# A selective-state recurrence with experts woven in: B and C are split 0.3 turns later, the experts' tiles are placed anew, and a product of zeros goes ahead of each state's sum

## The reference, cut to what matters

```python
xi, z = split(x @ in_proj.T)            # inner width 256 in layer 1
xc = silu(conv(xi))                     # over 4 steps of time
dt, B, C = split(xc @ x_proj.T)         # 8, 16 and 16 numbers per token
delta = softplus(dt @ dt_w.T + dt_b)
for t in time:                          # 16 states for each of 256 rows
    h = exp(delta[t] * A) * h + (delta[t] * xc[t]) * B[t]
    y[t] = sum_n h[:, n] * C[t, n]
out = ((y + xc * D) * silu(z)) @ out_proj.T
# experts: S = sigmoid(x @ Wg).T ; G, I = top_k(S, 1024)
# hid = gelu(x[I] @ W1 + b1) ; new_x[I] += (hid @ W2 + b2) * G
```

## Time and profile before

| | us |
|---|---|
| median of three runs | 4028.96 |
| profiled execution, own time | 4031.42 |
| its span, first to last instruction | 4030.1 |
| second layer's recurrence and experts | about 850 to 2207 |
| fourth layer's recurrence | about 2540 to 2900 |

### The profile page before, as it was taken

One profiled execution on the slowest core, in us unless ns is written; L12 is line 12 of the kernel. 1 busy time (PEld: TensorE's weight loads), 2 busy tenths in 40 slices (PEclk: granted clock), 3 DMA queues, 4 the chain that ended last, 5 costly groups with the idle time before them and its releaser, 6 DMA issues.

```text
span 4030.1 us, 40714 instructions
## 1 busy us (share of the span) xinstructions
PE 3097.7 (77%) x14760; PEld 1359.4 (34%) x14850; DVE 2581.5 (64%) x2891; ACT 2028.4 (50%) x3628; POOL 1557.2 (39%) x938
## 2 busy tenths in 40 slices
PE   5788877975567777777775879777687888888876
PEld 2111212341222222232322644322234554554544
DVE  4676662439998888888787334577625655555563
ACT  1454453134456766766664211576435565555654
POOL 2211100113457667666657002244414443443432
PEclk7788897986778888887777979888698998999998
DMA  3221200021111221121111001001000000000000
GB/s 86 41 33 30 45 3 0 0 75 39 26 35 37 42 51 32 40 49 36 32 34 45 1 0 64 21 21 32 11 0 19 19 19 10 19 19 10 19 10 31
DMA packets 79733, 114.60 MB, mean 28 GB/s; under 512 B 16270, under 2 KB 49422, under 8 KB 78106
## 3 DMA queue, kind: packets, MB, share of 16 engines
q1 hardware_dynamic: 68268, 103.33, 10.7%
q0 software_dynamic: 11264, 8.66, 1.6%
HBM read 37.96 MB, written 17.33 MB: 14 GB/s over the span
## 4 chain that ended last, share of the span: by engine, by line
PE 49%; DVE 21%; ACT 16%; issue 7%; POOL 3%; DMA 2%; SPq 1%; POOLq 0%; DVEq 0%; ACTq 0%
DVE layer_mamba_state L1340 7%; PE psum L1112 3%; DVE psum L1328 3%; PE psum L2460 3%; ACT layer_mamba_decay L1266 3%; PE psum L1189 3%; PE psum L2491 3%; PE psum L779 2%; ACT layer_exps L792 2%; PE psum L236 2%; PE psum L248 2%; PE psum L2154 2%; PE psum L905 2%; PE psum L242 2%; PE psum L2544 2%
## 5 line engine op out<-in xcount | busy, mean ns | idle before, releaser
L1369 POOL TENSOR_TENSOR layer_mamba_state<-layer_mamba_state,layer_mamba_c 128x1024 f32<-128x1024 f32 x320 | 781.0, 2450 | 591.3 <-DVE layer_mamba_state L1340 585.1
L1340 DVE TENSOR_TENSOR_SCAN layer_mamba_state<-layer_mamba_decay,psum 128x1024 f32<-128x1024 f32 x320 | 731.4, 2286 | 43.7 <-ACT layer_mamba_decay L1266 11.5
L1189 PE MATMUL psum<-layer_mamba_state,two_to_one 128*64 128x512 f32 x1280 | 442.9, 784 | 124.1 <-DVE layer_mamba_x L1357 80.9
L1266 ACT ACTIVATE layer_mamba_decay<-layer_mamba_delta_wide,layer_weights 128x511 f32<-128x511 f32 x640 | 415.7, 711 | 76.1 <-DMA layer_mamba_delta_wide<-layer_mamba_delta 39.5
L1328 DVE TENSOR_TENSOR psum<-psum,layer_mamba_u_wide 128x1024 f32<-128x1024 f32 x320 | 393.3, 1229 | 62.0 <-PE psum L1147 26.0
L720 DVE TENSOR_REDUCE layer_peak<-psum 128x2 f32<-128x1024 f32 x256 | 306.6, 1218 | 112.7 <-PE psum L691 108.6
L792 ACT ACTIVATE layer_exps<-psum 128x1024 f32<-128x1024 f32 x256 | 250.8, 1029 | 222.6 <-PE psum L759 222.6
L2857 POOL TENSOR_TENSOR layer_p<-layer_p,layer_stats 128x512 f32<-128x512 f32 x128 | 133.2, 1041 | 299.0 <-DVE layer_stats L2780 298.8
L2651 ACT ACTIVATE layer_p<-psum,layer_stats 128x128 f32<-128x128 f32 x512 | 181.5, 369 | 130.1 <-DVE layer_stats L2773 129.6
L2844 POOL TENSOR_TENSOR layer_qk<-layer_qk,layer_v_between 128x1024 f32<-128x1024 f32 x64 | 150.5, 2351 | 216.1 <-DVE layer_v_between L2744 214.3
L1147 PE MATMUL psum<-layer_mamba_bc,layer_mamba_pick 96*64 96x512 bf16 x768 | 164.2, 455 | 87.5 <-DVE psum L1328 63.7
(11 more groups left out here) (349 smaller groups left out, 6185.8 us busy)
## 6 DMA issues: line engine op xcount, KB each, us to landing
layer_mamba_delta_wide<-layer_mamba_delta SPq DMA_DIRECT2D x160, 128.0 KB, 2.4
layer_mamba_u_wide<-layer_mamba_work SPq DMA_DIRECT2D x160, 128.0 KB, 2.4
layer_v_between<-layer_v SPq DMA_DIRECT2D x16, 512.0 KB, 4.3
qk_dram<-layer_qk_parts SPq DMA_DIRECT2D x16, 384.0 KB, 3.0
layer_q_rows<-qk_dram SPq DMA_DIRECT2D x96, 64.0 KB
layer_k_rows<-qk_dram SPq DMA_DIRECT2D x96, 64.0 KB
layer_v_between<-layer_v SPq DMA_DIRECT2D x16, 384.0 KB, 5.6
layer_weights<-weights_dram SPq DMA_DIRECT2D x1, 4147.0 KB, 12.2
```

The source lines that it names most:

```text
L1189: e = pe.matmul(c.psum[j * HALF:(j + 1) * HALF, self.sum_banks[h], :], c.two_to_one[:, :], self.state[i % len(self.state)][:, j, :], start ...
L1266: e = act.activation(decay[:, j, 1:SEQ], self.delta_wide[h][:, j, 1:SEQ], ACT.Exp, scale=rates[:, rate:rate + 1])
L1340: dve.tensor_tensor_scan(state, decay, self.fill.rearrange("p j t -> p (j t)"), 0.0, ALU.mult, ALU.add).then_inc(self.scanned, 1)
L1369: pool.tensor_tensor(state, state, self.both(self.c_wide[turn % self.C_BUFFERS][:, :]), ALU.mult).then_inc(self.multiplied, 1)
```

## The change: what it does

Three edits, all of them in the order and in one added product.

1. In the second layer's plan `split`, `cast` and `rest` go from 4.75, 4.9, 5.05 to 5.05, 5.2, 5.4 turns. The fourth layer's plan keeps its numbers.
2. `ROWS_AT`, `TURN_AT`, `PAIR_AT` and `GIVE_AT` have new numbers (and `COUNT_AT` differs in the second decimal place). The last `GIVE_AT` is 1047.75 in place of 1037.75, and with it all gates are planned 10 us later.
3. `pe_keep_up` issues, ahead of each item's sum and ahead of its wait, a bf16 product of a 128x128 tile of zeros with a column of zeros read 512 times. It accumulates into a sum bank that is open (a unit's first item has none open and gets no product): 240 in the second layer, 56 in the fourth, where the class is used too. POOL clears `zeros16` once at the start.

```diff
+        pool.memset(c.zeros16[:, :], 0.0).then_inc(made, 1)
+        c.constants = 17
...
         for turn, h, i, now in self.items(self.plan.sum):
             yield now
             unit, m = divmod(turn, TURNS)
+            self.pe_keep_up()
             hold.wait_ge(self.multiplied, i + 1)
...
             e.then_inc(self.summed, 1)
+            self.open[h] = m < TURNS - 1
+
+    def pe_keep_up(self):
+
+        if any(self.open):
+            self.c.pe.matmul(self.c.psum[:, self.sum_banks[self.open.index(True)], :], self.c.zeros16[:, :],
+                             self.c.zeros16[:, 0:1].broadcast_to([P, SEQ]), start=False, stop=False)
...
-    ... z_gate=3.8, proj=4.2, keep=4.5, split=4.75, cast=4.9, rest=5.05, dt=4.9,
+    ... z_gate=3.8, proj=4.2, keep=4.5, split=5.05, cast=5.2, rest=5.4, dt=4.9,
...
-TURN_AT = [214.5, 264.5, 314.5, 370.75, 420.75, 470.75, ...
+TURN_AT = [214.5, 264.5, 314.5, 370.75, 432.0, 482.0, ...
```

More of the change, by code:

```diff
@@ L180, in __init__ @@
         buf = lambda n, s, d=F32: c.buffer(c.ctx, n, s, d)
-        c.ident, c.ident16 = buf("ident", [P, P]), buf("ident16", [P, P], BF16)
+        c.ident, c.ident16, c.zeros16 = buf("ident", [P, P]), buf("ident16", [P, P], BF16), buf("zeros16", [P, P], BF16)
         c.mean_of, c.eps = buf("mean_of", [P, P]), buf("eps", [P, 1])
@@ L202, in pool @@
         pool.tensor_tensor(c.two_to_one[:, :], c.ident[:, 0:P // 2], c.ident[:, P // 2:P], ALU.add).then_inc(made, 1)
-        c.constants = 16
+        pool.memset(c.zeros16[:, :], 0.0).then_inc(made, 1)
+        c.constants = 17
         hold.wait_ge(made, c.constants - 1)
@@ L1012, in __init__ @@
         self.halves, self.taps, self.units, self.names = halves, taps, units, names
-        self.plan, self.banks, self.sum_banks = plan, banks, sum_banks
+        self.plan, self.banks, self.sum_banks, self.open = plan, banks, sum_banks, [False] * halves
         self.fill = c.psum[:, fill_bank:fill_bank + 2, :]
@@ L1401 @@
     start=48.0, pace=8.3, item=3.75, first=0.55, spread=-4.2, c_spread=-2.8, copy=-1.8, decay=-6.0,
-    conv=((2.45, 2.63), (2.81, 2.99)), x=(2.9, 3.22), z=3.5, z_gate=3.8, proj=4.2, keep=4.5, split=4.75, cast=4.9, rest=5.05, dt=4.9,
+    conv=((2.45, 2.63), (2.81, 2.99)), x=(2.9, 3.22), z=3.5, z_gate=3.8, proj=4.2, keep=4.5, split=5.05, cast=5.2, rest=5.4, dt=4.9,
     soft=5.15, log=5.75, u=(6.15, 6.35), send_delta=(6.5, 6.6), send_u=(7.17, 7.62), multiply=3.9, sum=16.0, y=1.6, gate=1.78,
     back=2.0, out=2.3)
-ROWS_AT = [30.0, 34.0, 38.0, 42.0, 46.0, 50.0, 54.0, 58.0]
-COUNT_AT = [12.0, 18.3, 24.6, 30.9, 37.2, 43.5, 49.8, 56.1, 62.4, 69.7, 78.0, 84.3, 94.6, 100.9, 107.2, 113.5, 119.8]
+ROWS_AT = [30.0, 35.5, 39.5, 43.5, 47.5, 51.5, 55.5, 59.5]
+COUNT_AT = [12.0, 18.3, 24.6, 30.90, 37.2, 43.5, 49.8, 56.09, 62.39, 69.69, 77.99, 84.29, 94.59, 100.89, 107.19, 113.49, 119.79]
 SPOT_AT = COUNT_AT[15] + 16.0
@@ L1409 @@
 LIST_AT = [141.75, 158.25, 167.25, 176.25, 185.25, 194.25, 208.0, 224.75]
-TURN_AT = [214.5, 264.5, 314.5, 370.75, 420.75, 470.75, 520.75, 570.75, 628.0, 678.0, 728.0, 778.0, 835.5, 885.5, 935.5, 985.5]
-PAIR_AT = [232.75, 242.75, 297.25, 307.25, 325.0, 363.75, 377.0, 387.0, 430.0, 440.0, 496.5, 506.5, 525.25, 562.75, 576.25, 586.25, 632.5, 642.5, 695.75, 705.75, 762.0, 772.0, 789.75, 828.5, 842.0, 852.0, 894.75, 904.75, 961.25, 971.25, 990.0, 1027.75]
-GIVE_AT = [252.75, 317.25, 373.75, 412.25, 450.0, 516.5, 572.75, 611.5, 652.5, 715.75, 782.0, 838.5, 877.0, 914.75, 981.25, 1037.75]
+TURN_AT = [214.5, 264.5, 314.5, 370.75, 432.0, 482.0, 532.0, 582.0, 636.5, 697.75, 747.75, 802.5, 852.5, 902.5, 963.25, 1013.25]
+PAIR_AT = [232.75, 242.75, 297.25, 307.25, 325.0, 363.75, 377.0, 387.0, 436.5, 446.5, 496.5, 506.5, 562.75, 572.75, 590.5, 629.25, 642.75, 652.75, 702.25, 712.25, 762.0, 772.0, 828.5, 838.5, 857.0, 894.75, 908.25, 918.25, 967.75, 977.75, 1027.75, 1037.75]
+GIVE_AT = [252.75, 317.25, 373.75, 429.0, 456.5, 516.5, 582.75, 639.25, 694.5, 722.25, 782.0, 848.5, 904.75, 960.0, 987.75, 1047.75]
 class Setup1:
```

## The result

The changed kernel took 4046.73 us (median of seven, 4040.64 to 4048.79), the kernel before 4026.98 in seven of its own. The ratio is 1.0041, 95% interval 1.003 to 1.0052: slower by 0.41%, some 17 us. I had forecast 4037 with a range of 4004 to 4060. The profiled execution has a span of 4047.4 us against 4030.1. All times here are medians of each kernel's executions. The kernel before had medians of 4027 to 4033 us in the series that follow, so kernels are compared by their ratio to it.

What follows compares the result with a forecast made beforehand. Twelve 78.0 us units were taken as bound by an engine-to-engine chain (42.6 us), then DVE (about 35). Terms 13 + 4 - 5 - 3 - 1 = +8 on the median of 4028.96 gave 4037, range 4004 to 4060.

Steps and rivals of the forecast that it cites:

- Chain and second part: Each of twelve 78.0 us second-layer units: 42.6 us engine-to-engine chain from gate to delta, then about 35 us bound by DVE.
- Split: Second layer's split of B and C: fill L1328 moves into L1302's wait; nothing gained in steady units, -1 us allowed elsewhere.
- Fill comes through: Rival, chance 0.12: L1314's wait is set by DVE's own earlier work through a buffer, so -15 us, 4022.
- Zeros on the chain, +13: Second layer, gate to delta: three products of zeros a unit cost 1.07 us, +13 over twelve units.
- Zeros elsewhere, 0: Other eight or so products of zeros a unit run beside DVE's part, in PE's 9.7 us idle; cost 0.
- Zeros and the clock, -3: PE's two idle stretches a unit: one in twenty-four stays warm through the zeros, saving 2.6 us, so -3.
- Experts placed anew, -5: Experts' pieces L1704: at ends of units 5, 9, 13 they may keep the clock up, -3; pieces leaving the chain, -2.
- Tail, +4: Recurrence's end, bound by POOL: last piece and experts' gates planned 10 us later; +4 us, bounds 0 and +10.
- Fourth layer, 0: Its 56 products of zeros cost 0, bounds -2 and +4; PE waits for ACT ahead of dt there.
- Clock held: Rival, chance 0.20: half of the 24 cold PE stretches turn warm, -31 in place of -3, 4009.
- PE late in DVE's part: Rival, chance 0.15: zeros delay spreads behind the delta, +26 us, 4063; sign: L1337 waits for L1148 in the second part.
- POOL's backlog: Rival, chance 0.13: POOL's blocked fetch of 17.46 us moves to another unit, prolonging it by slow L1316s; +8, 4045.

## Why the prediction was right, and where it was not

The forecast was slower by 8 us, it became 17, inside a wide range. That the number held is in part luck, for the place was wrong. My terms put +5 us into the twelve chains (zeros +13, clock -3, boundaries -3, pieces that leave -2) and nothing into the second parts; measured are +1.7 and +14.6. By the sign that I had set myself, the second part moving from 35 us, the forecast's account is wrong: its mean went from 35.2 to 36.5. By its steps:

- **Chain and second part.** The division carried the whole study: the twelve units hold 16.2 of 17.3 us.
- **Split.** Right. The fill ran in L1302's wait (3.2 to 1.7 us a unit) and about half of it came back in L1314's (2.5 to 3.2, where I had 3.7). "Fill comes through" is out: with the new tables and no zeros the chain is 1.5 us shorter with the moved split than without it, not 15, and the ratio shows nothing.
- **Zeros on the chain, +13.** Right with the new tables: 501.4 to 514.1 is +12.7. With the old ones it is +6.1, so the hit is not the proof of a fixed price of three products a unit. The single product was mis-sized a little: at the lower clock the next row starts after 0.54 us (1390.07 to 1390.61), not 0.43:

```profile
1390.07 0.61 PE L1199 MATMUL psum<-zeros 128*128 128x512 bf16 x1
1390.61 1.98 PE L1191 MATMUL psum<-layer_mamba_state,two_to_one 128*64 128x512 f32 x4
```

- **Zeros elsewhere, 0.** Wrong, in the kernel's favour: -9.5 us on the kernel before. I had priced them as work and not as something that keeps the clock up where PE was only 72% busy. With the new tables the second part's zeros gave 11.5, and the chain's took 9.4 of it back, which no term of mine had.
- **Zeros and the clock, -3.** About right: two starts of a unit beside the three boundaries had their first sum at the upper level, no pair of dt products had. But the count of 24 cold stretches was wrong: in units 5, 8 and 12 before, pieces filled the idle ahead of dt, PE had no wait there and all stood at the upper level. The new tables took these pieces away.

```profile
1387.17 1.12 PE L1140 MATMUL psum<-layer_mamba_proj,layer_weights 8*128 8x512 f32 x2
...
1389.82 1.12 PE L1140 MATMUL psum<-layer_mamba_proj,layer_weights 8*128 8x512 f32 x2
```

- **Experts placed anew, -5.** This is the step that failed. The -5 was for the chain, and there it was right in sign: the chain fell by 9.5 us with the tables alone, and the clock was up at all three boundaries (I gave one in three). Such a start takes 1.08 + 1.98 us in place of 1.97 + 3.43, 2.3 us less and not 2.6. But I followed only what the pieces leave and where they fill, and not who waits for them where they arrive. In DVE's part "PE's work only if a fill has to wait for it" was to count; but DVE's L1908 stands in the queue too, 8.4 planned us behind the first piece, and this piece waits for a bank. That was +16.5 us, so +7 in the traces in place of -5 (+4 by the ratio).
- **Tail, +4.** The last period, from the thirteenth of these gates to the last one, was 58.1 and is 58.4: 0.
- **Fourth layer, 0.** Right.
- **Rivals.** "Clock held" did not happen at dt in the changed kernel: dt's products took 2.00 us on the mean (1.76 before). The reason given against it was the right one, shown by the fillers that do touch the idle. "PE late in DVE's part" did not happen by its sign: L1337's waits for L1148 went from 24 to 29 and from 25.7 to 42.5 us, but all 29 lie in the chain. They go with the chain's zeros: 27 waits of 27.2 us without zeros, 28 of 41.0 with zeros in the chain alone. DVE did wait for PE in the second part, but at L1908. "POOL's backlog" moved from unit 11 (5.18) to unit 5 at about the same price:

```profile
1488.34 5.50 DVE L1325 TENSOR_TENSOR layer_mamba_work<-layer_mamba_delta,layer_mamba_x 128x512 f32<-128x512 f32 x1
```

The sum was 9 us short of the result: 12 us for the tables by the traces, less the 4 of the tail. The zeros nearly cancel: 12.7 on the chain with what they did to the clock, where 10 stood, and -2 in the second part.

## What to carry to other kernels

When work is moved into a part that has idle time on its engine, look up the bank or buffer it must wait for and the instruction that waits for it: the engine that bounds the part stands in its own queue behind that. In this kernel filler products paid where they filled an idle stretch nearly to its end, or in a part that another engine bounds, and cost 6 to 13 us on the chain. With the zeros taken off the chain, twelve fillers a unit put into the idle ahead of dt, and one waiting instruction of three tiles moved back by an item, the change went from 17 us slower to 36 us faster. Split each period at the point where the bound changes and sum each half by itself: in the kernel without zeros the total showed -11 and +17 us as one small number. Test an edit on both sides of the other: here the zeros gained 9 us on the old tables and cost 15 on the new.

## What was not expected of the hardware

The clock behind an idle stretch is not the same from kernel to kernel. With the tables alone PE was idle for 5.65 us ahead of the first of the three tiles and was up again by 1408, within the third piece:

```profile
1400.49 2.08 PE L1704 MATMUL psum<-layer_expert,layer_hidden 128*128 128x128 f32 x8 [5.65 <-ACT layer_mamba_c L1276]
...
1408.05 1.06 PE L1704 MATMUL psum<-layer_expert,layer_hidden 128*128 128x128 f32 x8
```

The changed kernel's PE, idle for only 5.11 us, stayed at the lower level from 1403 to beyond 1417, with much the same instructions. The granted clock shows a difference ahead of the pieces. First with the tables alone, then in the changed kernel (columns as in the earlier trace rows):

```profile
1393.00:1407.10 14.10, 8.45 (x30) 4.65 (x26) 10.65 (x8) 11.25 (x17) 5.48 (x3) 0.50 0.18 41
1407.30:1415.00 7.70, 7.70 (x41) 4.25 (x42) 4.95 (x5) 3.05 (x6) 3.99 (x2) 1.00 0.25 58
```

```profile
1398.10:1401.40 3.30, 0.00 (x0) 0.00 (x0) 0.63 (x1) 3.27 (x6) 0.00 (x0) 1.00 0.00 0
1401.60:1418.40 16.80, 14.94 (x50) 9.73 (x52) 10.02 (x7) 5.87 (x10) 4.69 (x2) 0.50 0.27 62
```

With the tables alone the clock was down through the idle and rose once, under the pieces. In the changed kernel it rose in the idle, where no product could use it, fell again before the first piece and then stayed down for 16.8 us in which PE was busy for 14.9. The same rise and fall stands ahead of each of the three tiles in the changed kernel, in the one with zeros in the chain alone and in the one with L1908 later, and ahead of none in the three kernels without zeros in the chain (tables alone, no zeros, zeros in the second part). This is a good part of the difference between waits of 7.2 and 2.5 us. Why the clock then stays down for so long under steady work was not settled.

Products of zeros in a run start 0.22 us apart at the upper level: 11 of them take 2.56 us, the last 0.38 to its end. Between fp32 products the next row starts after 0.31.
